# First attention in f32: head pairs in two array halves, the mask added on DVE, byte masks by word logic, weight rows seeded by ACT

## What is computed

```
h = relu(layernorm(x));  x1 = x + mean over 8 heads of softmax(scores) @ h
q = h[sub] @ Wq.T + bq;  k = h[obj] @ Wk.T + bk            # 10000 pairs (sub, obj), nodes 0 to 1499
scores[head, sub, obj] = (q . k) / 8                       # heads of 64 features
scores where adj == 0: -inf;  elsewhere without a pair: 0;  diagonal: 1e-7
```

## Time and profile before

| | us |
|---|---|
| median of 3 runs (1420.40 to 1427.26) | 1424.48 |
| profiled execution, its time | 1427.51 |
| its span in the profile | 1426.0 |
| busy: PE / DVE / ACT / POOL | 1245.6 / 1063.6 / 764.6 / 306.5 |
| mean granted clock of TensorE | 0.947 |

### The profile page before, as it was taken

One profiled execution on the slowest core, in us unless ns is written; L12 is line 12 of the kernel. 1 busy time (PEld: TensorE's weight loads), 2 busy tenths in 40 slices (PEclk: granted clock), 3 DMA queues, 4 the chain that ended last, 5 costly groups with the idle time before them and its releaser, 6 DMA issues. The chain is left out here.

```text
span 1426.0 us, 26813 instructions
## 1 busy us (share of the span) xinstructions
PE 1245.6 (87%) x11026; PEld 839.5 (59%) x11026; DVE 1063.6 (75%) x1411; ACT 764.6 (54%) x763; POOL 306.5 (21%) x247
## 2 busy tenths in 40 slices
PE   4885066999999999989978948999999999999797
PEld 2442022344444444444434528999999999999743
DVE  4576047999999999986214978899898899898455
ACT  2221054454545444442213449899998999989122
POOL 2588643222223233300003630000000000000011
PEclk9998588999999999999998978999999999999999
DMA  6744132122222222212118640000110000100141
GB/s 260 217 116 134 17 70 52 48 68 68 68 68 68 68 48 54 51 27 59 45 41 219 105 105 31 32 31 32 53 40 32 31 32 32 61 32 2 52 148 74
DMA packets 81268, 99.61 MB, mean 70 GB/s; under 512 B 44401, under 2 KB 60032, under 8 KB 79120
## 3 DMA queue, kind: packets, MB, share of 16 engines
q1 hardware_dynamic: 71024, 69.91, 15.6%
q0 software_dynamic: 10144, 28.24, 9.5%
HBM read 88.20 MB, written 20.33 MB: 76 GB/s over the span
## 5 line engine op out<-in xcount | busy, mean ns | idle before, releaser
L990 ACT ACTIVATE s_masks<-s_s1b,s 128x2048 fp8e4<-128x2048 f32 x208 | 396.7, 1987 | 0.0
L1135 PE MATMUL psum<-s_V,s_masks 128*128 128x198 bf16 x2560 | 352.9, 249 | 15.1 <-DVE s_masks L1032 15.1
L1136 PE MATMUL psum<-s_V,nadjT 128*128 128x99 bf16 x2560 | 347.6, 209 | 0.0
L579 ACT ACTIVATE s_exp<-psum,s_negm 128x1536 f32<-128x1536 f32 x96 | 148.0, 1542 | 232.3 <-DVE s_W L648 184.9
L1135 PEld LDWEIGHTS psum<-s_V,s_masks 128*128 128x128 fp8e4 x2560 | 250.2, 98 | 15.7 <-issue 15.4
L1136 PEld LDWEIGHTS psum<-s_V,nadjT 128*128 128x128 fp8e4 x2560 | 250.5, 98 | 0.0
L518 PE MATMUL psum<-h,s_WT 128*128 128x512 f32 x512 | 240.6, 598 | 0.0
L640 DVE TENSOR_SCALAR_CACHE_REDUCE s_junkv<-psum 128x1536 bf16<-128x1536 f32 x96 | 168.5, 1755 | 57.2 <-PE psum L538 55.3
L1032 DVE TENSOR_TENSOR s_masks<-s_masks,adjT 128x512 uint32<-128x512 uint32 x256 | 169.4, 681 | 49.5 <-ACT s_masks L990 47.0
L535 PE MATMUL psum<-f_keys,f_q 128*128 128x512 bf16 x288 | 112.2, 390 | 88.0 <-PEq L221 58.7
L648 DVE SCALAR_TENSOR_TENSOR s_W<-s_exp,s_r,s_W 128x1536 f32<-128x1536 f32 x84 | 179.3, 2135 | 0.2
(11 more groups left out here) (141 smaller groups left out, 1620.8 us busy)
## 6 DMA issues: line engine op xcount, KB each, us to landing
s_s1b<-s_rows SPq DMA_DIRECT2D x16, 1024.0 KB, 4.7
f_q<-q_parts SPq DMA_DIRECT2D x72, 128.0 KB, 3.2
f_adj<-in_adj POOLq DMA_DIRECT2D x16, 512.0 KB, 5.2
s_adj<-in_adj POOLq DMA_DIRECT2D x16, 512.0 KB, 5.2
rel_planes<-s_zero POOLq DMA_DIRECT2D x3, 2304.0 KB, 19.2
f_rel<-rel_planes SPq DMA_DIRECT2D x36, 192.0 KB, 3.1
f_keys<-s_parts SPq DMA_DIRECT2D x48, 128.0 KB, 2.8
s_x<-x SPq DMA_DIRECT2D x6, 1024.0 KB, 12.3
```

Source lines behind the costliest of these rows:

```text
L579: act.activation(ex[:, hd, :], ps[:, 3 * (hd % 2):3 * (hd % 2) + 3, :].rearrange("p c j -> p (c j)"), ACT.Exp, bias=negm[:, b, hd:hd + 1], ...
L990: act.activation(masks[:, j, :], s1b[b][:, :], ACT.Relu, bias=t["s2"][:, n, 0, j:j + 1], scale=BIG, saturate=False).then_inc(signs, 1)
L1135: pe.matmul(out, masks[:, j, cols], V[:, b, j, :, :], **first)
L1136: last = pe.matmul(out[:, :, DZ:CZ], nadjT[:, j, cols], V[:, b, j, :, DZ:CZ], **then)
```

## The change

**Stage 1.** The split, the parts and their 60 stores are gone. ACT writes keys and queries as f32 straight into `f_qk` in SBUF. POOL issues four loads of the adjacency ahead of the scatters where there was one. Masks of the first two tiles are made here, where it was one.

**Scores.** Heads go in pairs. Head 2p has its 64 features in partitions 0 to 63 and head 2p+1 in 64 to 127. Each head takes three f32 matmuls 64x128 by 64x512 instead of twelve bf16 ones; the two heads alternate, and both write before the next pair may start (`masked`). There is no mask matmul.

**Mask and maximum.** One DVE instruction (`mask`) reads the scores and `low`, writes -(score + low) to `s_exp` in f32 and keeps the row's minimum. ACT's exponential then works in place in SBUF.

**Masks.** The adjacency, the planes and the mask are bytes (1.0 in fp8 is 0x38, which the scatters write). DVE joins the planes, clears the diagonal and separates pairs from neighbours by and, or and xor on 32-bit words. POOL computes nothing in stage 2.

**Weight rows.** ACT starts `W` as adjacency times the common weight (`start_w`); DVE adds the diagonal, then the eight heads. The passes L654 and L656 are gone.

**Order.** The loop is unrolled. DVE takes a finished tile out of PSUM at the start of step n+2 (`finish`), not at the end of step n+1, and joins the planes of tile n+2 right behind it. SP issues the load of those planes behind its wait for `summed`.

```diff
-        self.keys = sb("keys", [P, 2, HA, NE], BF16)
-        self.k1, self.k2 = self.keys[:, 0, :, :], self.keys[:, 1, :, :]
-        self.qs = [sb(f"q{i}", [P, 3, HA, P], BF16) for i in range(2)]
-        self.adjn = sb("adj", [P, 4, N], BF16)
+        self.qk = sb("qk", [P, 2, KT, NE])
+        self.adjn = sb("adj", [P, ADJ_RING, N], F8)
         self.rel = [sb(f"rel{i}", [P, PLANES, NE], U8) for i in range(2)]
-        self.scored = sb("scored", [P, NE], BF16)
+        self.scored = sb("scored", [P, NE], F8)
...
+    def clear_diagonal(self, dve, t, it):
+        own = self.adjn[:, it % ADJ_RING, it * P:(it + 1) * P].bitcast(U32)
+        dve.wait_ge(self.adj_in[it % ADJ_RING], 16 * (it // ADJ_RING + 1))
+        last = dve.tensor_tensor(own, own, t["offdiag8"][:, :].bitcast(U32), ALU.bitwise_and)
+        last.then_inc(self.cleared if it < ET else self.nbr_ready, 1)
+    def join_planes(self, dve, it):
+        rel = self.rel[it % 2]
+        dve.wait_ge(self.rel_in[it % 2], 16 * PLANES * (it // 2 + 1))
         for i in range(1, PLANES):
             if i > 1:
+                dve.wait_ge(self.joined, (PLANES - 1) * it + i - 1)
+            dve.tensor_tensor(rel[:, 0, :].bitcast(U32), rel[:, 0, :].bitcast(U32), rel[:, i, :].bitcast(U32),
+                              ALU.bitwise_or).then_inc(self.joined, 1)
+    def mark_related(self, dve, it):
+        near = self.adjn[:, it % ADJ_RING, 0:NE].bitcast(U32)
+        dve.wait_ge(self.joined, (PLANES - 1) * (it + 1))
+        dve.wait_ge(self.cleared, it + 1)
+        if it:
+            dve.wait_ge(self.low_ready, it)
+        dve.tensor_tensor(self.scored[:, :].bitcast(U32), self.rel[it % 2][:, 0, :].bitcast(U32), near,
+                          ALU.bitwise_and).then_inc(self.marked, 1)
+        dve.wait_ge(self.marked, it + 1)
+        dve.tensor_tensor(near, near, self.scored[:, :].bitcast(U32), ALU.bitwise_xor).then_inc(self.nbr_ready, 1)
...
-                    dve.tensor_copy(q[:, HI, :], v).then_inc(split_step, 1)
-                    dve.wait_ge(split_step, 3 * g + 1)
-                    dve.tensor_tensor(v, v, q[:, HI, :], ALU.subtract).then_inc(split_step, 1)
-                    dve.wait_ge(split_step, 3 * g + 2)
-                    dve.tensor_copy(q[:, MID, :], v).then_inc(split_step, 1)
-                    dve.wait_ge(split_step, 3 * g + 3)
-                    dve.tensor_tensor(q[:, LO, :], v, q[:, MID, :], ALU.subtract).then_inc(parts_ready, 1)
...
+            for it in range(ADJ_RING):
+                f.load_adj(pool, io, it)
...
+            for n in range(NT):
+                b = n % 2
+                if n + 2 < ET:
+                    sp.wait_ge(f.marked, n + 1)
+                    f.load_related(sp, t, n + 2)
+                if n >= 2:
+                    sp.wait_ge(y_out[b], 16 * (n // 2))
+                    sp.wait_ge(measured, n - 1)
+                sp.dma_start(xt[b][:, :], io["x"][n * P:(n + 1) * P, :]).then_inc(x_in[b], 16)
+                if n:
+                    sp.wait_ge(summed, n)
+                    sp.dma_start(t["x1"][(n - 1) * P:n * P, :], xt[1 - b][:, :]).then_inc(y_out[1 - b], 16)
...
+            def score(n, p):
+                if n or p:
+                    pe.wait_ge(masked, HA * n + 2 * p)
+                for ch in range(CH):
+                    for half in range(2):
+                        rows = slice(half * DK, (half + 1) * DK)
+                        last = pe.matmul(ps[:, 3 * half + ch, :], qk[rows, Q, p, n * P:(n + 1) * P],
+                                         qk[rows, K, p, ch * 512:(ch + 1) * 512], start=True, stop=True)
+                        if ch == CH - 1:
+                            last.then_inc(scores, 1)
...
+            def start_w(n):
+                act.wait_ge(fac, 6 * (n + 1))
+                if n >= 2:
+                    act.wait_ge(turned, HA * (n - 1))
+                act.activation(W[n % 2][:, :], adjn[:, n % ADJ_RING, :], ACT.Copy, scale=cd[:, 0:1]).then_inc(w_started, 1)
+            def count(n):
+                act.wait_ge(f.nbr_ready, n + 1)
+                if n >= 2:
+                    act.wait_ge(fac, 6 * (n - 1))
+                act.activation(adjn[:, n % ADJ_RING, :], adjn[:, n % ADJ_RING, :], ACT.Copy, saturate=False,
+                               accum_out=n0[:, n % 2:n % 2 + 1]).then_inc(rowsum, 1)
+            def exp(n, hd):
+                b = n % 2
+                act.wait_ge(masked, HA * n + hd + 1)
+                act.activation(ex[:, hd, :], ex[:, hd, :], ACT.Exp, bias=negm[:, b, hd:hd + 1], scale=-1.0,
+                               accum_out=zs[:, b, hd:hd + 1]).then_inc(exped, 1)
+            def turned_copy(n, m):
+                act.wait_ge(turned, HA * n + m + 1)
+                if n or m >= 2:
+                    act.wait_ge(agg, HA * n + m - 1)
+                act.activation(WT[m % 2][:, :, :], ps[:, 6, 0:2 * P].rearrange("p (b i) -> p b i", b=2),
+                               ACT.Copy).then_inc(turned_out, 1)
...
+            def add_diagonal(n):
+                own = W[n % 2][:, n * P:(n + 1) * P]
+                dve.wait_ge(fac, 6 * (n + 1))
+                dve.wait_ge(w_started, n + 1)
+                dve.scalar_tensor_tensor(own, t["ident"][:, :], cd[:, 1:2], own, ALU.mult, ALU.add
+                                         ).then_inc(diag_added if n < ET else w_ready, 1)
+            def add_head(n, hd):
+                dve.wait_ge(*((added, (HA - 1) * n + hd) if hd else (diag_added, n + 1)))
+                dve.scalar_tensor_tensor(W[n % 2][:, 0:NE], ex[:, hd, :], r8[:, hd:hd + 1], W[n % 2][:, 0:NE], ALU.mult,
+                                         ALU.add).then_inc(added if hd < HA - 1 else w_ready, 1)
+            def mask(n, hd):
+                dve.wait_ge(scores, HA * n + hd + 1)
+                dve.wait_ge(f.low_ready, n + 1)
+                if n:
+                    dve.wait_ge(*((added, (HA - 1) * (n - 1) + hd + 1) if hd < HA - 1 else (w_ready, n)))
+                dve.tensor_tensor_reduce(ex[:, hd, :], ps[:, 3 * (hd % 2):3 * (hd % 2) + 3, :].rearrange("p c j -> p (c j)"),
+                                         low[n % 2][:, :], -1.0, -DIAG, ALU.add, ALU.min,
+                                         accum_out=negm[:, n % 2, hd:hd + 1]).then_inc(masked, 1)
...
+            def step(n):
+                if n >= 2:
+                    finish(n - 2)
+                    measure(n - 2)
+                if 0 <= n < NT:
+                    if n + 2 < ET:
+                        f.join_planes(dve, n + 2)
+                    factors(n)
+                    if n + 2 < NT:
+                        f.clear_diagonal(dve, t, n + 2)
+                    if n + 2 < ET:
+                        f.mark_related(dve, n + 2)
+                    add_diagonal(n)
+                for p in range(PAIRS):
+                    for hd in (2 * p, 2 * p + 1):
+                        if 0 <= n < ET:
+                            add_head(n, hd)
+                    for hd in (2 * p, 2 * p + 1):
+                        if n + 1 < ET:
+                            mask(n + 1, hd)
```

More of the change, by code:

```diff
@@ L123, in load_related @@
+        self.adj_in = [sem(f"adj_in{i}") for i in range(ADJ_RING)]
+        self.joined, self.cleared, self.marked, self.nbr_ready, self.low_ready, self.big_set = (
+            sem("joined"), sem("cleared"), sem("marked"), sem("nbr"), sem("low"), sem("big_set"))
     def load_related(self, sp, t, it):
         for i in range(PLANES):
-            sp.dma_start(self.rel[it.par()][:, i, :], t["rel_planes"][i][it.rows(), :]).then_inc(self.rel_in[it.par()], 16)
+            sp.dma_start(self.rel[it % 2][:, i, :], t["rel_planes"][i][it * P:(it + 1) * P, :]).then_inc(self.rel_in[it % 2], 16)
@@ L127, in load_adj @@
     def load_adj(self, pool, io, it):
[L128 to L140 removed]
+        r = it % ADJ_RING
@@ L341, in _ @@
             norm(2)
-            copy(8, 12)
-            split(0, 4)
-            copy(12, 16)
-            split(4, 8)
+            copy(8, 16)
             norm(3)
             copy(16, 20)
-            split(8, G)
-            f.mark_related(dve, At(0, 0), first=True)
+            for it in range(2):
+                f.clear_diagonal(dve, t, it)
+                f.join_planes(dve, it)
+                f.mark_related(dve, it)
         @block.scalar
@@ L378, in _ @@
             act.wait_ge(f.big_set, 1)
-            f.make_low(act, At(0, 0))
+            for it in range(2):
+                f.make_low(act, it)
         @block.tensor
@@ L423, in stage2 @@
     h = t["h"]
-    qs, adjn, low = f.qs, f.adjn, f.low
+    Q, K = 0, 1
+    qk, adjn, low = f.qk, f.adjn, f.low
     ex = sb("s2_exp", [P, HA, NE])
@@ L520, in aggregate @@
                 last.then_inc(agg, 1)
[L522 to L546 removed]
+            def step(n):
+                for p in range(PAIRS):
+                    if n + 1 < ET:
+                        score(n + 1, p)
+                    if n > 0:
```

(29 more changed lines are left out.)

334 lines of the change are left out of this document (77 added, 257 removed).

## The result

The kernel after the change takes **1475.49 us** (median of 4 runs, 1474.6 to 1476.66) against 1423.41 (4 runs): a ratio of **1.0343**, 95% interval 1.0312 to 1.0374. It is slower, as forecast, by 52 us where 34 were expected, and inside the range. The profiled execution took 1474.6 us, its span 1473.1, 47.1 more than the span before.

What follows compares the result with a forecast made beforehand. DVE and PE were taken as both near their limit, DVE leading. Terms -7.0, +15.1, -2.4, +33.5 (tail) and -5.6 sum to +33.6 on 1427.5: 1461, less 3.0 for the median: 1458 us; range 1430 to 1545.

Steps and rivals of the forecast that it cites:

- Halves of the array: PE's scores: a head pair's matmuls run in both array halves at once, taking 2.6 us rather than 5.15.
- rival A: PE's scores: the halves take turns, a pair takes 9.05 us, a tile 46.4, the kernel 1540; chance 0.13.
- Two-source mask: DVE's mask per head: one instruction reading two sources takes 1.68 us from start to start.
- rival C: DVE's mask: two sources cost a second pass, 3.3 us and not 1.7, the kernel 1610; chance 0.05.
- Planes: Head of each tile: DVE idles 3.8 us for plane loads; join may start 5.5 us after `finish` starts.
- Last aggregate: Ahead of the next `finish`: DVE waits 2.2 us for PE, as ACT's last copy follows head 6's exponential.
- First score to first sum: Steps -1 to 1, before the first finished tile: 103.2 us against 110.2, a gain of 7.0 us.
- 4.35 between 2.6 and 5.15: Step -1: a pair's scores, each after a pause at low clock, taken as 4.35 us; four pairs 31.5.
- The tail: Last tiles: aggregates wait 6.2 us more for weight rows and count, 1.6 for low clock; 24.0 us, without count 22.2.
- Stage 1: Start to first score: 3.6 us earlier after planes, up to 6.9 less scattering, more adjacency loads; together -5.6 us.
- Rival B: Head of a tile: its waits are covered, a tile costs DVE's own 33.2 us, the kernel 1392; chance 0.14.
- Rival D: Start, tail and stage 1: clock stays up, stage 1 gains its most, plane loads short; about 1432 us; chance 0.06.

Runs made afterwards that it cites:

- the blocked order: Changed kernel with a head pair's six score matmuls issued as three of one array half, then three of the other: 1506.3 us, one run.
- planes early: Changed kernel with SP issuing the planes of tile n+3 once tile n+2 is marked, ahead of its wait for the summed tile: 1447.5 us.
- weight rows moved late: Changed kernel with ACT, from tile 12 on, starting weight rows only behind the fourth copy of turned rows and counting behind the sixth: 1443.9 us.
- PE kept busy: On top of all four edits together, PE fills its pauses in steps -1 and 0 with matmuls nobody reads: 1363.1 us, ratio 0.9579.
- all four edits together: Changed kernel with planes loaded early, earlier turning and aggregating on PE, weight rows late in the tail, adjacency loads behind the scatters: 1377.4 us, ratio 0.9685.

## Why the prediction was right in sign and 17 us short

The mechanism was named as it is: DVE's busy time for a tile fell to about 33 us, and what was hidden came to stand at the head of each tile. Point by point:

- **Halves of the array.** Taken at 2.6 us, measured 2.77. Right; rival A is out, and even the blocked order, in its one run, cost 31 us and not its 82.
- **Two-source mask.** Taken at 1.68 from start to start, measured 1.68; the additions 1.85 and 1.74 taken, 3.58 for two measured; never slowed by another engine. Right; rival C is out.
- **Planes.** Forecast 3.8 us of idling a tile, measured 4.1 (join 5.75 us after the sum, not 5.5). The theory behind it, that SP's order and not chance removes the slack, is shown by planes early. Right.
- **Last aggregate.** Forecast 2.2, measured 2.37, but for the wrong reason. So the 2.2 was luck. The step that failed is "ACT copies the last turned rows only after the exponential of head 6": taking that away shortened the wait by 0.3 us and the kernel by nothing. PE's 8.6 us against DVE's 6.9 in the last pair stood behind it. The forecast had checked PE's share of a pair as an average (2.6 + 3.9, inside 6.95), and the last pair has one aggregate more.
- **The low clock in repeated tiles.** Not in the sum: the second pair's scores at 1.2 GHz made DVE wait 0.9 us in three tiles of eight, 2.7 us in all. The other 1.9 us by which this stretch was short are 0.2 a tile: 0.25 more for the planes, 0.17 for the aggregate and 0.15 for the weight rows (2.15 us from the factors to the diagonal), less most of the 0.3 that the sum had for signals.
- **First score to first sum.** The step mis-sized is "4.35 between 2.6 and 5.15". The rows show 5.5 and 4.5 by turns, to the mask's start 5.6 and 4.6:

```profile
180.54 5.49 PE L440 MATMUL psum<-f_qk 64*128 64x512 f32 x12 [61.48 <-PEq L203]
...
189.64 4.54 PE L440 MATMUL psum<-f_qk 64*128 64x512 f32 x12 [3.61 <-DVE s_negm L593]
```

In steps -1 to 1 DVE waits 26.4 us for scores. Step -1 took 34.3 us against 31.5. Step 0 took 37.7 against 36.0: the forecast gave its pairs 30.6 us, 2.8 above DVE's own 27.8, though PE pauses 3.5 to 7.3 us ahead of three of them, runs their scores largely at the low clock, and DVE waits 3.8 us for them. Step 1 with its wait took 36.8 against 35.5. The forecast's terms add up to 103.0, not to the 103.2 that it carries, and its 7.87 for a pair is 4.35 and two masks (7.71) with a rest that it does not name. All this is 5.5 of the 13.5 us that the sum was short, and the run with PE kept busy shows the cause.
- **The tail.** Mechanism and size right: three steps at 24.2 us on average for the 24.0 forecast. PE's pause ahead of the first aggregate is 6.5 us and the four instructions behind it take 3.62. The weight rows moved late take all of it away in steps 12 to 15. (The forecast's 2.6 + 1.9 + 2.0 + 0.4 is 6.9, not 6.8.) Step 11 took 25.4 against 24.0 and step 15 23.0 against 22.2; these 2.2 us were not taken apart.
- **Stage 1.** -5.0 against -5.6, but by other parts: the scatters' busy time fell by the full 6.9 us (101.3 to 94.4, the mean from 1266 to 1180 ns), but the fourth scatter's wait behind four loads grew by 8.7, from 2.3 to 11.0, two later waits of 4.0 together went away, and in the end the last scatter came only 1.1 us earlier. The other 3.9 us lie behind it, for the 3.6 forecast. The forecast had the loads' cost hidden "beside the zeroing"; it is not.
- **The rest** of the 17: 3 us were taken off because the profiled execution before lay 3 above its median; after the change it lies 0.9 below.

**Rival B** was a statement of what the change could be worth, and all four edits together reach it: 33.92 us a tile against the 33.2 of its sum, and 1377 us, even below its 1392, since stage 1 and the tail had more to give. Its price and place were right, its condition (that the waits are covered) was not met by the change as it stands. **Rival D** is out: the clock falls in steps -1 to 1, in the repeated tiles and in the tail (granted 0.75, 0.86 and 0.86, where the kernel before had 0.90, 1.00 and 0.97). As it stands the change costs 52 us; with its order mended it gains 43 on the kernel before, and 14 more with PE kept busy at the start.

Not tried: whether the planes' loads themselves could be shortened, and which of the four edits the kernel before, with its old arithmetic, would itself gain from. So the 43 us are what the change and the four edits give together; how much of them is the change's own is not shown.

## What to carry to other kernels

When a change cuts the work of the leading engine, write down for the new step which transfers and copies are issued behind a signal of that same step, since those become its length. Compare engines pair by pair rather than by a tile's mean: one stage with an extra piece decides who waits. And fill an engine's forced pause with its own later work before removing a wait elsewhere, because here a pause of PE was paid for twice, the second time as matmuls at half the clock.

## What was not expected of the hardware

- The low clock is dear where many short pauses follow each other: in steps -1 and 0 matmuls that serve nothing but to fill pauses of 3.5 us raised the granted clock up to the first sum from 0.75 to 0.96 and made the kernel 14 us faster.
- Two heads in the two halves of the array, interleaved instruction by instruction, run 1.86 times as fast as an estimate of them in turn (2.77 against 12 x 0.43 = 5.15 us). In blocks of six instructions they keep part of that, 3.74: the second block starts 0.97 us behind the first, ahead of three of the first block's instructions.
- With four adjacency loads issued ahead of it on the same engine, the first scatter was signalled 9.8 us later than with one (the fourth scatter, which waits for it, starts at 54.6 and not 44.8). Queue and traffic were not told apart.
- A shortened wait can put the low clock where it costs more: with the planes early a tile is 3.3 us shorter and the granted clock of the repeated tiles is 0.86 as ahead of it, but their second pair of scores is at 1.2 GHz in all tiles and not in three of eight.
